# Two-layer gated cross-attention with routed experts: first weights of two expert blocks split ahead, second block's rows turned early, last block in halves

## The reference

```python
# layer 0: 8 experts, the two best of each token, softmax of the two logits as weights
h = gelu(xf @ W1[e] + b1[e]);  y = h @ W2[e] + b2[e]      # W1 256x1024, W2 1024x256
x = x + tanh(g_ffn[0]) * sum over the chosen e of comb[n, e] * y[n, e]
# layer 1: 7 experts and a no-op; the first 256 tokens of each expert's list
h = relu(inputs @ experts_inter[e]);  out = (h @ experts_out[e]) * in_w
x = x + tanh(g_ffn[1]) * (scatter-add of out + x * noop_w)
```

## Time and profile before

| what | us |
|---|---|
| median of 3 timed runs | 925.03 |
| these runs | 922.13, 925.03, 925.53 |
| the profiled execution, its own time | 927.32 |
| its span in the trace | 925.6 |
| experts of layer 0 in the trace | about 263 to 554 |
| experts of layer 1 in the trace | about 820 to 925.6 |

### The profile page before, as it was taken

How to read it: one execution, slowest core, us unless ns; L and a number is a source line. 1 busy time by engine, 2 the same in 40 slices (tenths; PEclk the granted TensorE clock), 3 DMA queues, 4 the chain that set the end, 5 groups by cost and what they waited for, 6 DMA issues and landing times. The chain is left out here.

```text
span 925.6 us, 17977 instructions
## 1 busy us (share of the span) xinstructions
PE 785.1 (85%) x7040; PEld 669.9 (72%) x7040; DVE 629.6 (68%) x1193; ACT 468.4 (51%) x694; POOL 424.2 (46%) x404
## 2 busy tenths in 40 slices
PE   5889999988338999999999956789999897438995
PEld 5656667656338999999999956666677655338995
DVE  3567776642568999999999823667776732658882
ACT  2246656643036777777777622256666543325541
POOL 8433554111234777777777339334553112232653
PEclk8979999989658999999999986979999989559998
DMA  5211121110166788878877335211221110675732
GB/s 185 65 38 37 42 77 50 44 48 24 46 244 228 228 239 244 241 242 240 242 243 239 81 35 180 61 36 37 63 63 48 40 47 24 183 195 195 228 83 33
DMA packets 57140, 113.75 MB, mean 123 GB/s; under 512 B 14176, under 2 KB 43360, under 8 KB 49376
## 3 DMA queue, kind: packets, MB, share of 16 engines
q0 software_dynamic: 20256, 69.43, 26.8%
q1 hardware_dynamic: 36800, 43.18, 15.4%
HBM read 85.17 MB, written 18.75 MB: 112 GB/s over the span
## 5 line engine op out<-in xcount | busy, mean ns | idle before, releaser
L441 DVE TENSOR_REDUCE mx_a<-ps_max_a 128x2 f32<-128x512 f32 x256 | 164.4, 684 | 64.6 <-PE ps_max_a L615 62.7
L71 PE MATMUL ps_h_e<-xe_t_e,w_e 128*128 128x256 f32 x480 | 141.0, 294 | 9.9 <-DVE xe_t_e L1360 9.9
L372 ACT ACTIVATE prob_a<-ps_st_a 128x2048 f32<-128x2048 f32 x64 | 120.0, 1876 | 54.9 <-PE ps_st_a L636 54.9
L72 PE MATMUL ps_h_e<-xe_t_e,w_e 128*128 128x256 f32 x480 | 137.7, 287 | 0.0
L73 PE MATMUL ps_h_e<-xe_t_e,w_e 128*128 128x256 f32 x480 | 137.4, 286 | 0.0
L71 PE MATMUL ps_y_e<-w_e,h_e 128*128 128x256 f32 x480 | 132.8, 277 | 0.0
L73 PE MATMUL ps_y_e<-w_e,h_e 128*128 128x256 f32 x480 | 132.8, 277 | 0.0
L72 PE MATMUL ps_y_e<-w_e,h_e 128*128 128x256 f32 x480 | 132.7, 276 | 0.0
L71 PEld LDWEIGHTS ps_h_e<-xe_t_e,w_e 128*128 128x128 f32 x480 | 95.2, 198 | 11.1 <-DVE xe_t_e L1360 11.1
L270 POOL TENSOR_SCALAR r_var_eps_a<-r_mean_var_a 128x2 f32<-128x2 f32 x16 | 3.6, 228 | 211.9 <-DVE r_mean_var_a L468 211.9
L1204 POOL DMA_INDIRECT xe_e<-normalised_weighted,token_of x60 | 79.0, 1317 | 46.7 <-POOLq L59 19.7
(11 more groups left out here) (211 smaller groups left out, 1800.8 us busy)
## 6 DMA issues: line engine op xcount, KB each, us to landing
w_raw_w<-L_w SPq DMA_DIRECT2D x14, 1024.0 KB, 5.6
ctx_raw_a<-ctx_t SPq DMA_DIRECT2D x16, 256.0 KB, 3.0
q_s_a<-q_c_a SPq DMA_DIRECT2D x128, 32.0 KB, 2.0
k_s_a<-k_c_a SPq DMA_DIRECT2D x128, 32.0 KB, 2.0
normalised_weighted<-xr SPq DMA_DIRECT2D x16, 256.0 KB, 2.3
x_sb<-x SPq DMA_DIRECT2D x2, 1792.0 KB, 10.2
x<-x_sb SPq DMA_DIRECT2D x8, 256.0 KB, 2.5
out<-x_sb SPq DMA_DIRECT2D x8, 256.0 KB, 2.5
```

The costliest lines, as they stand in the source:

```text
L71: pe.matmul(out, lhs[0], rhs[0], start=start, stop=False)
L72: pe.matmul(out, lhs[1], rhs[0], start=False, stop=False)
L372: act.activation(prob[n % 2][:, :, :, :], ps_st[:, :, :, :], ACT.Exp, scale=HD ** -0.5).then_inc(prob_ready, 1)
L441: dve.tensor_reduce(mx[:, q, h + 2 * j:h + 2 * j + 2], ps_max[j][:, :, :], AX.X, ALU.max).then_inc(max_done, 1)
```

## The change

In both layers, ACT and DVE split `w1` of blocks 0 and 1 before the first inputs arrive, and no longer split `w1` of block 1 within block 0. The rows of block 1 are turned after piece 0 of `first_product(0)` and no longer after piece 2, and their split on ACT and DVE moves from piece 3 to piece 1. In layer 0 one Gelu of 128 values is evaluated ahead, on a value that nothing reads. From block 1 on the order is as before. The last block of each layer runs its second product, bias or weight, and scatter by halves of 128 slots, the second half in the other PSUM bank; the semaphores `last_ps`, `last_biased` and `last_ready` count its halves.

```diff
@@ add_to_tokens (POOL)
-                pool.wait_ge(y_ready, b + 1)
+                if b < blocks - 1:
+                    pool.wait_ge(y_ready, b + 1)
                 if b:
                     pool.wait_ge(y_out[(b - 1) % 2], loaded(b - 1, QT))
...
                 for q in range(QT):
                     t = b * QT + q
+                    if b == blocks - 1:
+                        pool.wait_ge(last_ready, q + 1)
                     pool.indirect_dma_start(
@@ weigh (ACT)
                 for q in range(QT):
+                    if b == blocks - 1:
+                        act.wait_ge(last_biased, q + 1)
                     ins = act.activation(y[b % 2][:, q, :], y_raw[b % 2][:, q, :], ACT.Copy, scale=slot_weight[:, b, q:q + 1])
+                    if b == blocks - 1:
+                        ins.then_inc(last_ready, 1)
@@ ACT's loop
-            for k in range(KC):
-                w1_high(0, k)
+            for b in range(2):
+                for k in range(KC):
+                    w1_high(b, k)
+            if layer == 0:
+                act.activation(unread[:, :], shared["tanh_g"][:, 0:1], ACT.Gelu)
             inputs_high(0)
             for b in range(blocks):
                 for jp in range(NP):
                     if jp < KC:
-                        if b + 1 < blocks:
+                        if b and b + 1 < blocks:
                             w1_high(b + 1, jp)
                     else:
                         w2_high(b, jp - KC)
-                    if jp == NP - 1 and b + 1 < blocks:
+                    if jp == (NP - 1 if b else 1) and b + 1 < blocks:
                         inputs_high(b + 1)
@@ DVE's loop: w1_low and inputs_low in the same way
+            def last_output(b):
+                if layer:
+                    dve.wait_ge(y_out[b % 2], loaded(b - 2, QT))
+                else:
+                    dve.wait_ge(y_ready, b - 1)
+                for q in range(QT):
+                    dve.wait_ge(last_ps, q + 1)
+                    if layer:
+                        dve.tensor_scalar(y[b % 2][:, q, :], ps_y[(b + q) % 2][:, q, :], slot_weight[:, b, q:q + 1], None,
+                                          ALU.mult).then_inc(last_ready, 1)
+                    else:
+                        dve.tensor_tensor(y_raw[b % 2][:, q, :], ps_y[(b + q) % 2][:, q, :], b2[b % 2][:, :], ALU.add).then_inc(last_biased, 1)
@@ first_product (PE)
-                    if jp == NP - 2 and b + 1 < blocks:
+                    if jp == (NP - 2 if b else 0) and b + 1 < blocks:
                         turn(b + 1)
@@ second_product (PE)
                 for q in range(QT):
+                    bank = ps_y[b % 2]
+                    if b == blocks - 1 and q:
+                        wait(pe, y_ready if layer else y_biased, b)
+                        bank = ps_y[(b + 1) % 2]
...
+                    if b == blocks - 1:
+                        ins.then_inc(last_ps, 1)
```

More of the change, by code:

```diff
@@ L1161, in expert_phase @@
             by_expert = sb("by_expert", [P, QT, E])
-            picked, y_biased = sem("picked"), sem("y_biased")
+            unread = sb("unread", [P, 1])
+            picked, y_biased, last_biased = sem("picked"), sem("y_biased"), sem("last_biased")
         ps_x = [ps(f"ps_x{i}", [P, KC, SB]) for i in range(2)]
@@ L1171, in expert_phase @@
                              "hid_ready", "h_hi", "h_ready", "y_ps", "y_ready"))
+        last_ps, last_ready = sem("last_ps"), sem("last_ready")
         NP = FC // 2
@@ L1275, in weigh @@
             def weigh(b):
-                act.wait_ge(y_biased, b + 1)
+                if b < blocks - 1:
+                    act.wait_ge(y_biased, b + 1)
                 if b >= 2:
@@ L1279, in weigh @@
                 for q in range(QT):
+                    if b == blocks - 1:
+                        act.wait_ge(last_biased, q + 1)
                     ins = act.activation(y[b % 2][:, q, :], y_raw[b % 2][:, q, :], ACT.Copy, scale=slot_weight[:, b, q:q + 1])
-                ins.then_inc(y_ready, 1)
+                    if b == blocks - 1:
+                        ins.then_inc(last_ready, 1)
+                if b < blocks - 1:
+                    ins.then_inc(y_ready, 1)
             def inputs_high(b):
@@ L1338, in output @@
             def output(b):
+                if b == blocks - 1:
+                    last_output(b)
+                    return
                 dve.wait_ge(y_ps, b + 1)
@@ L1361, in inputs_low @@
                                   ALU.subtract).then_inc(xe_ready, 1)
-            for k in range(KC):
-                w1_low(0, k)
+            for b in range(2):
+                for k in range(KC):
+                    w1_low(b, k)
             inputs_low(0)
@@ L1408, in second_product @@
                 for q in range(QT):
+                    bank = ps_y[b % 2]
+                    if b == blocks - 1 and q:
+                        wait(pe, y_ready if layer else y_biased, b)
+                        bank = ps_y[(b + 1) % 2]
                     for j in range(FC):
-                        ins = split_matmul(pe, ps_y[b % 2][:, q, :], [h[b % 2][s][:, j, q * P:(q + 1) * P] for s in range(2)],
+                        ins = split_matmul(pe, bank[:, q, :], [h[b % 2][s][:, j, q * P:(q + 1) * P] for s in range(2)],
                                            [w2[b % 2][s][:, j, :] for s in range(2)], j == 0, j == FC - 1)
-                ins.then_inc(y_ps, 1)
+                    if b == blocks - 1:
+                        ins.then_inc(last_ps, 1)
+                if b < blocks - 1:
+                    ins.then_inc(y_ps, 1)
             turn(0)
```

## The result

The changed kernel takes 919.72 us, the median of 14 executions, beside 924.49 of the kernel before (14 executions, 921.95 to 928.24). The ratio is 0.9948, with an interval of 0.9932 to 0.9964: 4.8 us faster (3.3 to 6.3). Of the 14 one took 1889.18 and is not looked at here; the others lie between 916.09 and 923.88. The forecast was 918.3 in a range of 915.0 to 922.5, from a gain of 6.7.

The account below looks back on a forecast made before the run. PE was taken as the bound, with DVE close behind. Gains of 5.1 us in layer 0, 1.6 in layer 1 and 0 for the halves summed to 6.7, from 925.03 to 918.3 us; whole range 915.0 to 922.5.

Parts of the forecast that it names:

- Layer 0: Experts of layer 0: wait before `first_product(1)` and clock fall go, new 1.2 us wait before the third first product; gain 5.1 us.
- No waits later: Layer 0 after block 2: DVE stays ahead of PE, by 0.3 us at block 3, widening 0.25 a block.
- DVE as the real bound: Rival: gain in front given back over layer 0's 21 later blocks, DVE cycle 11.8 us; about 924 us, chance 0.06.
- its casts in the long form throughout: Rival: DVE's casts take 0.66 us instead of 0.43, cycle 12.5; about 938 us, or 928 if half; chance 0.03.
- a clock that falls in the new wait: Rival: PE's clock falls in layer 0's new 1.2 us wait, costing 1.7 to 2.7; about 920.7 us, chance 0.08.
- Gain 1.6 us: Layer 1's experts: `first_product(2)` starts at 850.2 instead of 851.8; bounds of the gain about 1.1 and 3.1 us.
- PE now waits 1.6 us: Layer 1, within the first product of block 0: PE, at the turn at 830.4, waits for block 1's rows until 831.9.
- a rise 3.5 us after PE resumes: Layer 1, after PE's wait for block 1's rows: PE's clock goes back up at 835.5.
- layer 1 gives nothing or loses: Rival: block 1's rows land later or the clock comes late in layer 1; about 920.5 us, chance 0.14.
- the third load: Layer 1: SP's third `w1` load, now near 826, taken as harmless; slowing rows 2.6 us would lose 1 us.
- The rival on the halves: Last block: the landing of the scatter before comes earlier, 1 to 2 us more gain; 916.8 us, chance 0.03.
- The table load: Rival, layer 0: a pause as long as the load makes ACT 0.7 us late for the first inputs; 919.0 us, chance 0.04.

Follow-up runs that it names:

- e1: Kernel before, with the early splits and early turn in layer 0 alone, no Gelu ahead, no halves: 919.68 us, ratio 0.9946.
- e9: e5 with block 2's turn and inputs one piece earlier in both layers: 916.26 us, ratio 0.9915 to the kernel before.
- e10: e5 with block 0's `w2` split right behind the first inputs in both layers: 911.8 us, ratio 0.9857 to the kernel before.
- e3: Changed kernel with splits, turn and Gelu back where they were; halves and POOL's wait edits stay: 922.69 us, ratio 0.9969 to the kernel before.
- e4: Kernel before, with the order of POOL's two waits exchanged in the last block, no halves: 923.87 us, ratio 0.9981.
- e2: Kernel before, with the early splits and early turn in layer 1 alone: 925.5 us, ratio 0.9993.
- e8: Changed kernel without the Gelu evaluated ahead: one time, 922.13 us.
- e11: Changed kernel, halves kept, with POOL's two waits of the last block in the old order: one time, 919.65 us.
- e6: Changed kernel; in layer 1 DVE makes block 1's low weight parts behind the first inputs, which also delays SP's third load: one time, 914.86 us.
- e7: Changed kernel; SP issues its third weight load of layer 1 only when block 1's inputs are ready: one time, 919.53 us.
- e5: Changed kernel; SP's weight loads of layer 1 wait until block 1's rows have landed: one time, 916.35 us.

## Why the prediction was right, and where it was off

**Layer 0: right, size and mechanism.** The first matmul starts 7.85 us after the first copy (271.57 - 263.72; before 7.82), the wait ahead of `first_product(1)` and the fall of the clock are gone, and one wait for DVE took their place, 0.98 us for the 1.2 of the sum. The gain was put at 5.1. Up to PE's last output matmul layer 0 gives 5.27 in the changed kernel and 5.04 in e1. It has the two parts of the forecast: 3.75 - 0.98 = 2.8 us less of waiting, and 2.6 us less of busy time for the same matmuls at the higher clock. DVE is late there since it has no gap from 277.5 on, and e9 and e10 show that it is its work that counts: moving the deadline moves the wait, filling the gap ahead of it removes it.

**No waits later: right.** DVE's outputs start 11.22 us apart (293.44, 304.66), under PE's 11.54, and the page's group has no other wait. With it fall three rivals: DVE as the real bound, its casts in the long form throughout (one took 0.66, at 292.08; those at 288.79 and 303.59 took 0.42), and a clock that falls in the new wait. (In that last rival half of 3.7 to 5.7 us is 1.9 to 2.9, not 1.7 to 2.7; no chance hangs on it.)

**Layer 1: the step that failed.** The prediction wrote of it "Gain 1.6 us", from "they land at 831.9", "PE now waits 1.6 us", and "a rise 3.5 us after PE resumes". Measured: no gain. `first_product(1)` starts 12.77 us after the layer's first matmul (forecast 10.56, before 11.01), and `first_product(2)` 24.20 (forecast 22.56, before 24.19). From one execution to another this moves: PE's last output matmul ends 95.0 to 95.6 us after the first copy in the four profiles with the old order at the start of layer 1 (before, e1, e3, e4), and 95.3 to 96.3 in four with the new one and SP as it was (after, e2, e8, e11). A small loss is as well borne out as none. The forecast and the changed kernel, taken apart:

- The four gathers took 5.00 us from first to last issue, not 4.03 (824.73 - 820.70 before, 818.50 - 813.50 after). The third took 1.91 instead of 0.95 beside the longer run of DVE's weight subtracts; e6 takes that run away, and it is 0.95 again. The last section says which gather is hit. The prediction counted what DVE does ahead of the inputs as free, because nobody waits for DVE; the issues of another engine were longer beside it.
- The time from issue to landing was taken as the 7.2 of before. It was about 7.7 after (from PE's start, see e6), and 7.8 in e8 and e11: another 0.5.
- PE asked for the rows 0.1 us later than in the sum (2.93 us after the first matmul, not 2.80). Together: 831.95 - 830.44 is 1.5, and 1.5 + 0.97 + 0.5 - 0.1 gives the 2.90 measured.
- The clock rose 5.0 us after PE resumed, 1.5 later than taken; at half rate that is 0.7 us of work. It is the least steady term: 4.6, 4.7 and 5.8 in e7, e11 and e8, and in e2 it rose before PE resumed and fell again.

1.3 for the wait and 0.7 for the clock are 2.0 of the 2.2 by which `first_product(1)` is late. In the forecast `first_product(2)` then waited 0.45 for DVE (849.75 and 850.2); PE now comes later and finds DVE done, and 1.64 is left, the whole of the gain. The rival "layer 1 gives nothing or loses" had a chance of 0.14, and it is what came, for both of its reasons, later rows and a late clock. Only the suspect named there, the third load, is cleared by e7. This agrees with the rule that the prediction took from the Trainium skill, "DMA: Bandwidth & Descriptors", section "Queues, rings and completion order": a load behind two others of its own queue does not come between the rows (8.2 without it, 7.8 with it). What slows the rows is the first two: with all three held back the landing takes 2.8 (e5), and 4.1 us of the layer go with the change. e5 removes PE's wait although the third gather is still long, and e6 most of it although the two loads are still there.

**Halves: a small term missed.** It stood at 0, as POOL waits for a landing whichever way the output comes. POOL does so still, and the halves themselves give nothing (e11). But the edit also turned round POOL's two waits, which the prediction counted as "one more wait for POOL, under 0.1". The order is worth 0.46 us in layer 0 and 0.45 in layer 1, as 0.73 less 0.27 from the landing to the next scatter also says. What POOL or its queue does in that time the trace does not show, and it stays open. The rival on the halves wanted an earlier landing and 1 to 2 us; it falls.

**The table load.** The copies end at 267.63, the load takes 1.28, and the Gelu starts at 268.92: no pause behind it. The Trainium skill's "ScalarE: Activation LUTs", section "What ACT_TABLE_LOAD costs", has 1.38 us of drain beside the load. The changed kernel shows none on either side of it, and the measurement decides; with the load in its old place there is none ahead of it, and a pause behind would lie in the wait for PE (e8). The rival falls.

**The sum.** Forecast were 5.1 + 1.6 + 0 = 6.7. By phase it is 5.3 for layer 0's PE, about -0.2 for layer 1's, and 0.5 for each of the two tails: 6.1. So the 1.8 us that layer 1 did not give were made up in part by the 1.0 of POOL's waits, which the sum did not have. The timed 4.8 (3.3 to 6.3) is 1.9 below the forecast's gain; 0.6 of that is the phases', and the rest is no more than the interval allows. That the forecast comes within 1.4 us of the measured time is in part luck: a term of 1.6 that did not come and one of 1.0 that was not foreseen have opposite signs. Each of e1 (5.0) and the whole change (4.8) timed alone can't tell 5.3 from 6.1.

## What to carry to other kernels

A wait that is removed at the start of a phase is worth its own length and the clock that it cost, until the next engine is late: count that engine's work from the moment at which it has no gap left, and fill the gap ahead of it (e10), for reordering within it only moves the wait. When a consumer is moved ahead, ask of the transfer it needs who else moves data at that time, and hold back what is not urgent (e5: one wait on SP, 4.1 us). An edit that "only" splits work can also change the order of waits, and here the effect hung on that order.

## What the runs showed of the hardware

- An indirect gather on POOL takes 0.95 us to issue, but one that starts while DVE runs a weight subtract (TENSOR_TENSOR, both inputs in SBUF, 1.22 us) ends no sooner than 0.82 us after the end of that subtract. After, in layer 1, the third gather starts at 816.29, 0.13 us into a subtract of 816.16 to 817.38, and ends at 818.20; the fourth starts at 818.50, 0.02 us before the last subtract ends, and takes 0.95. Before, the gather of 827.86 meets a subtract of 827.77 to 828.99 and ends at 829.81. So it is not the length of DVE's run that counts, but which gather starts inside a subtract and how early in it. Over the 13 profiles 657 gathers of rows and weights start inside a weight subtract, and 643 of them end within 0.07 us of that time, or of their own 0.95 where it is later; the other 14 start in its first 0.01 us and take 0.95. All 281 that take over 1.5 us start inside one. A gather that meets the inputs' subtract, which reads PSUM, takes 0.95 with 0.58 us of it still to run.
- Rests of PE of 0.5 to 1.8 us at 2.4 GHz did not bring the clock down. Those of 2.8 to 3.8 us did, eight times in the profiles of before and e1 to e4, 2.4 to 2.8 us after PE stopped. One of them is in layer 1 before (the clock is low from 838.3 to 841.7), of which the prediction does not speak. In layer 1 of e2 PE rested 2.96 us, the clock being up for the last 2.2 of them, and it fell 1.2 us after PE resumed. After a rest at the low level the clock took 4.6 to 5.8 us to rise (after, e7, e8, e11).
- With a landing and an output to wait for, POOL started its scatter 0.27 us behind the landing when it waited for the landing first, and 0.73 to 0.75 behind it when it waited for it last (4.05 and 4.08 us from the scatter before, against 4.51 and 4.53).
